# Layers' orders with seven stretches of tiled matmuls an item and two sets of squares, and a first attention with later loads and foldings among the scores

## The reference

```
xn = layernorm(x)
# branch 1: attention over all 512 tokens, 16 heads of 8 channels, interleaved rotary
q, k = rope(xn @ Wq.T), rope(xn @ Wk.T);  v = xn @ Wv.T
a = softmax(q k^T / sqrt(8)) v
# branch 2: six layers on y = xn
for i in range(6):
    # local attention: 16 heads of 64, windows of 32 queries that see 64 keys
    q, k, v = split(shift(y) @ Wqkv[i])        # shift: half of the channels one token later
    q, k = rotary(l2norm(q) * qs), rotary(l2norm(k) * ks)
    y = local_softmax(8 q k^T, masked) v @ Wo[i] + y
    # feed forward: layer norm, gelu gate, hidden size 341
    h = layernorm(shift(y)) * g + b
    y = (h @ W1a + b1a) * gelu(h @ W1g + b1g) @ W2[i] + b2 + y
out = x + a + y
```

## Time and profile before

| what | value |
|---|---|
| median of three runs | 3385.4 us |
| the profiled execution | 3384.84 us |
| its span, first to last instruction | 3383.0 us |
| granted TensorE clock, mean | 0.978 |
| first attention, to the layers' first load | 0 to 485.4 us |
| layers | 485.4 to 3383.0 us |

### The profile page before, as it was taken

The page is one execution under the profiler, slowest core; times in us unless marked ns, Lnnn a source line. Parts: engine busy times, 40 slices in busy tenths (PEclk is TensorE's granted clock), DMA queues, the critical chain, the costliest instruction groups (busy, mean ns, idle before and its releaser), DMA issues.

```text
span 3383.0 us, 96906 instructions
## 1 busy us (share of the span) xinstructions
PE 3228.3 (95%) x39772; PEld 1496.3 (44%) x39772; DVE 2841.0 (84%) x3719; ACT 1766.0 (52%) x2636; POOL 2647.8 (78%) x1918
## 2 busy tenths in 40 slices
PE   6899976899999999999999999999999999999988
PEld 4333232444444444444444444444444444444443
DVE  6899936888888888888888888888888888888863
ACT  2578853455555555545555555555555555555542
POOL 3223217999899999999999989989989999888961
PEclk7899997999999999999999999999999999999999
DMA  7333122333333333333333333333333333333321
GB/s 215 83 62 65 39 95 70 84 79 80 86 84 92 85 79 78 94 77 92 84 80 86 84 90 86 80 81 89 81 90 85 80 86 82 90 84 79 79 64 53
DMA packets 200487, 283.38 MB, mean 84 GB/s; under 512 B 56561, under 2 KB 82417, under 8 KB 199153
## 3 DMA queue, kind: packets, MB, share of 16 engines
q1 hardware_dynamic: 196304, 262.75, 31.6%
q10 hardware_dynamic: 3744, 14.43, 1.2%
HBM read 44.30 MB, written 19.55 MB: 19 GB/s over the span
## 4 chain that ended last, share of the span: by engine, by line
PE 78%; SPq 2%; POOL 2%; DVE 1%; issue 1%; DMA 1%; ACT 1%; DVEq 0%; POOLq 0%
PE ly_pj_ps L1005 20%; PE ly_to_ps L1081 20%; PE ly_pair_ps L1069 11%; PE ly_pair_ps L1049 9%; PE ly_to_ps L1111 4%; PE ly_pair_ps L1099 4%; PE ly_pair_ps L1103 3%; PE ly_nq_ps L1015 3%; PE ly_pair_ps L1036 2%; SPq L914 1%; PE ly_pair_ps L1089 1%; PE ly_pair_ps L1058 1%; SPq L904 1%; PE ly_pair_ps L1029 1%; DMA ly_kp<-ly_kr 0%
## 5 line engine op out<-in xcount | busy, mean ns | idle before, releaser
L1206 DVE SCALAR_TENSOR_TENSOR ly_prod<-ly_pj_ps,ly_few,ly_tables 128x1024 f32<-128x1024 f32 x768 | 964.9, 1272 | 149.4 <-ACT ly_sq L1403 132.2
L1005 PE MATMUL ly_pj_ps<-ly_xs,ly_wqk 128*128 128x512 f32 x1536 | 802.0, 625 | 30.6 <-DVE ly_prod L1206 14.8
L1081 PE MATMUL ly_to_ps<-ly_u,ly_mvo 128*128 128x512 f32 x1536 | 763.8, 606 | 0.9 <-issue 0.7
L1403 ACT ACTIVATE ly_sq<-ly_pj_ps 128x512 f32<-128x512 f32 x768 | 451.4, 603 | 574.7 <-PE ly_pj_ps L1005 494.1
L1499 POOL TENSOR_TENSOR ly_sq<-ly_sq 128x512 f32<-128x512 f32 x384 | 488.1, 1278 | 119.1 <-ACT ly_sq L1403 118.2
L1503 POOL TENSOR_TENSOR ly_sx<-ly_sx,ly_smax 128x1024 f32<-128x1024 f32 x192 | 365.7, 1905 | 126.0 <-DVE ly_smax L1282 125.5
L1434 ACT COPY ly_u<-ly_pair_ps 128x1024 f32<-128x1024 f32 x384 | 369.4, 1013 | 133.0 <-PE ly_pair_ps L1069 133.0
L1005 PEld LDWEIGHTS ly_pj_ps<-ly_xs,ly_wqk 128*128 128x128 f32 x1536 | 266.8, 192 | 347.7 <-issue 236.9
L1049 PEld LDWEIGHTS ly_pair_ps<-ly_kp,ly_qp 64*32 64x32 f32 x24576 | 277.4, 106 | 281.3 <-issue 242.6
L1081 PEld LDWEIGHTS ly_to_ps<-ly_u,ly_mvo 128*128 128x128 f32 x1536 | 272.6, 190 | 276.2 <-issue 262.9
L1069 PE MATMUL ly_pair_ps<-ly_pt,ly_xt 32*128 32x512 f32 x3072 | 385.3, 615 | 9.5 <-ACT ly_u L1434 6.8
(11 more groups left out here) (125 smaller groups left out, 4232.4 us busy)
## 6 DMA issues: line engine op xcount, KB each, us to landing
ly_qp<-ly_qr SPq DMA_DIRECT2D x1536, 64.0 KB
ly_kp<-ly_kr SPq DMA_DIRECT2D x1536, 64.0 KB, 2.0
ly_xt<-ly_xt SPq DMA_DIRECT2D x48, 192.0 KB
ga_parts_dram<-ga_parts SPq DMA_DIRECT2D x16, 384.0 KB, 2.4
ga_qs<-ga_parts_dram SPq DMA_DIRECT2D x96, 64.0 KB
ga_ks<-ga_parts_dram SPq DMA_DIRECT2D x96, 64.0 KB
ly_wqk<-in_wqk SPq DMA_DIRECT2D x24, 256.0 KB, 3.8
ly_mvo<-mvo_dram SPq DMA_DIRECT2D x24, 256.0 KB, 3.8
```

The source lines that it names most:

```text
L1005: pe.matmul(pj_ps[:, j % 2, :], wqk[:, g, j % TILES, :], xs[:, n % 2, WIN:], start=True, stop=True).then_inc(proj_ready.sem, 1)
L1081: last = pe.matmul(to_ps[:], mvo[:, 4 * (h // 4) + BESIDE[h % 4], :], u[:, :, :, h, :].rearrange("p t c q -> p (t c) q"), start=(h == 0), ...
L1206: dve.scalar_tensor_tensor(prod[:, k], pj_ps[:, j % 2, :].unsqueeze(1).to_broadcast([P, 2, N]), gains[:, n // B, k:k + 1], tables[:, table ...
L1403: act.activation(sq[:, k, :], pj_ps[:, j % 2, :], ACT.Square).then_inc(sq_done.sem, 1)
```

## The change

In the first attention, the load of items 4 to 7 (`load_x(2)`) moves from the start to behind item 0's stacking, and the raw weights of layer 1 are loaded by ACT only when item 0's stacked rows have landed. The items' normalising, turning and copying is split: items 1 to 3 in body 0, items 4 to 7 in body 1. The early foldings 4 to 15 move from body 0 (and 11 to 15 from body 1) to places among `first` of item 0 in body 1. The late foldings 17 to 23 stand among the scores of item 7 in body 9; before, 18 to 23 stood in body 10 after them. The store of an item's sum moves behind the late stores, and POOL waits for a group of x only where it adds it.

```diff
@@ first attention, SP
-            load_x(2)
...
+            def load_last_x(n):
+                if n == 0:
+                    load_x(2)
...
-                take_maxima(x_1, 0); stack(x_0, 1); store_sum(x_2); store_late(x_2, 0); store_late(x_2, 1)
+                take_maxima(x_1, 0); stack(x_0, 1); load_last_x(x_0); store_late(x_2, 0); store_late(x_2, 1); store_sum(x_2)
@@ first attention, PE (early and late foldings and the turns of the items)
+            def turn_group(n, g):
...
+                fold(x_0, 0); out(x_3, 3)
...
+                fold(x_0, 1); first(x_1, 3); second(x_2, 6); first(x_1, 4); meet(x_2, 1, 0); fold(x_2, 17); second(x_2, 7)
...
+                first(x_1, 5); meet(x_2, 1, 1); second(x_2, 8); first(x_1, 6); fold(x_1, 4); meet(x_2, 2, 0); second(x_2, 9)
+                fold(x_0, 2); fold(x_0, 3); turn_group(x_0, 1)
+                first(x_1, 7); fold(x_1, 5); meet(x_2, 2, 1); first(x_1, 8); fold(x_1, 6); second(x_2, 10); meet(x_2, 3, 0)
...
+                first(x_1, 9); fold(x_1, 7); out(x_2, 0); fold(x_2, 18); fold(x_2, 19); second(x_2, 12); first(x_1, 10)
+                turn_group(x_1, 2); meet(x_2, 4, 0)
...
+                meet(x_2, 5, 0); meet(x_2, 5, 1); fold(x_2, 20); first(x_1, 13); fold(x_1, 8); second(x_2, 15); meet(x_2, 6, 0)
...
+                fold(x_1, 9); second(x_2, 16)
+                meet(x_2, 6, 1); first(x_1, 15); fold(x_1, 10); second(x_2, 17); meet(x_2, 7, 0); meet(x_2, 7, 1); first(x_1, 16)
+                fold(x_1, 11)
+                second(x_2, 18); first(x_1, 17); meet(x_2, 8, 0); second(x_2, 19); out(x_2, 1); fold(x_2, 21); second(x_2, 20)
...
+                meet(x_2, 9, 0); fold(x_2, 22); fold(x_2, 23); second(x_2, 22); first(x_1, 20); meet(x_2, 9, 1)
...
+                second(x_2, 25); first(x_1, 23); fold(x_1, 12); meet(x_2, 11, 0); second(x_2, 26); first(x_1, 24); fold(x_1, 13)
...
+                first(x_1, 25); fold(x_1, 14); second(x_2, 28); first(x_1, 26); fold(x_1, 15); meet(x_2, 12, 0)
...
+                first(x_1, 27); meet(x_2, 13, 0); fold(x_1, 16); meet(x_2, 13, 1); second(x_2, 30); first(x_1, 28)
@@ first attention, ACT
-            load_raw(1)
...
+            def load_second_raw(n):
+                if n != 0:
+                    return
+                act.wait_ge(stacked[0].sem, stacked[0].at(0, 16 * 4 * len(TERMS)))
+                load_raw(1)
+
+                exponentials(x_2, 3, 4); take(x_3, 3); exponentials(x_2, 5, 6, 7, 8, 9, 10, 11, 12, 13, 14, 15)
+                gain_early(x_0, 0); take_early(x_0, 0); copy_values(x_0); take_early(x_0, 1); take_early(x_0, 2)
+                copy_group(x_0, 1)
+                load_second_raw(x_0); pass_on(x_0, 0)
+                gain_early(x_1, 1); take_early(x_1, 3); take_early(x_1, 4); take_early(x_1, 5); pass_on(x_1, 1)
+                copy_group(x_1, 2)
...
@@ first attention, DVE
...
+                maxima(x_1, 3, 4, 5, 6, 7, 8, 9); normalise_group(x_1, 2); take_late(x_2, 1); gain_late(x_2, 0); output(x_2, 0)
+                take_late(x_2, 2); gain_late(x_2, 1); take_late(x_2, 3); normalise_group(x_0, 1)
+                maxima(x_1, 10, 11, 12, 13, 14, 15, 16, 17); output(x_2, 1); take_late(x_2, 4); take_late(x_2, 5); maxima(x_1, 18)
...
@@ layers: two sets of squares (buffer, square_sums, squares, add_squares)
-        sq = sb("sq", [P, TILES, N])
+        sq = sb("sq", [P, 2, TILES, N])
+                        last = pe.matmul(nq_ps[32 * t:32 * t + 32, 0:P], heads[:, g, side, :], sq[:, g % 2, 2 * side, t * P:(t + 1) * P],
-                    if k == 0 and UNITS * n + g:
-                        act.wait_ge(ns_ready.sem, UNITS * n + g)
-                    act.activation(sq[:, k, :], pj_ps[:, j % 2, :], ACT.Square).then_inc(sq_done.sem, 1)
+                    if k == 0 and UNITS * n + g >= 2:
+                        act.wait_ge(ns_ready.sem, UNITS * n + g - 1)
+                    act.activation(sq[:, g % 2, k, :], pj_ps[:, j % 2, :], ACT.Square).then_inc(sq_done.sem, 1)
+                    side, at = k // 2 % 2, 2 * (k % 2)
+                    pool.tensor_tensor(sq[:, side, at], sq[:, side, at], sq[:, side, at + 1], ALU.add).then_inc(sq_added.sem, 1)
```

More of the change, by code:

```diff
@@ L428, in body @@
[L428 to L431, removed]
@@ L673, in _ @@
             pool.memset(ks[:].bitcast(F32), ONE_PAIR).then_inc(ks_set, 1)
-            for g in range(len(GROUPS_LN)):
-                pool.wait_ge(x_in[g], 16)
             def cut_sums(n, i):
@@ L707, in add_tokens @@
                     return
+                for g, (first, _) in enumerate(GROUPS_LN):
+                    if n == first:
+                        pool.wait_ge(x_in[g], 16)
                 pool.wait_ge(out_steps.sem, out_steps.at(n, 8))
@@ L1182, in body @@
+                if x_6 is not None: turn_ffn_tokens(x_6)
+                if x_7 is not None: up_value(x_7, 2); down(x_7, 1)
+                if x_3 is not None: project(x_3, 10)
+                if x_5 is not None: attend(x_5, 2)
+                if x_3 is not None: square_sums(x_3, 1); project(x_3, 11, 12)
+                if x_5 is not None: attend(x_5, 3)
+                if x_3 is not None: project(x_3, 13)
                 if x_7 is not None: down(x_7, 2)
-                if x_5 is not None: attend(x_5, 2)
@@ L1184, in body @@
-                if x_3 is not None: square_sums(x_3, 2); project(x_3, 12, 13)
-                if x_5 is not None: attend(x_5, 3)
-                if x_3 is not None: project(x_3, 14)
                 if i == ITEMS + 5: turn_back(0, 1)
@@ L1349, in body @@
                 if x_7 is not None: normalise(x_7)
+                if x_5 is not None: prob_sums(x_5, 2); inverse_sums(x_5, 2)
+                if i == ITEMS + 6: add_sums(2)
                 if x_3 is not None: products(x_3, 1)
+                if x_4 is not None: scale_keys(x_4, 1)
+                if x_5 is not None: prob_sums(x_5, 3); prob_blocks(x_5, 2); inverse_sums(x_5, 3)
+                if x_3 is not None: products(x_3, 2)
+                if x_7 is not None: gated(x_7, 0)
+                if x_3 is not None: products(x_3, 3)
@@ L1351, in body @@
+                if x_7 is not None: gated(x_7, 1)
+                if x_4 is not None: scale_keys(x_4, 2)
                 if i == ITEMS + 6: add_sums(3)
-                if x_4 is not None: scale_keys(x_4, 1)
-                if x_5 is not None: prob_sums(x_5, 3); inverse_sums(x_5, 3); prob_blocks(x_5, 2)
-                if x_7 is not None: gated(x_7, 0)
-                if x_3 is not None: products(x_3, 2)
                 if x_5 is not None: prob_blocks(x_5, 3)
-                if x_7 is not None: gated(x_7, 1)
@@ L1368, in body @@
[L1368 to L1372 removed]
+                if x_3 is not None: products(x_3, 9)
+                if x_6 is not None: token_moments(x_6)
+                if x_3 is not None: products(x_3, 10)
+                if x_4 is not None: prob_sums(x_4, 0)
@@ L1376, in body @@
-                if x_3 is not None: products(x_3, 12)
+                if x_4 is not None: mask_scores(x_4, 2); score_maxima(x_4, 2)
+                if x_3 is not None: products(x_3, 14, 15)
             bodies(body)
@@ L1457, in body @@
-                if x_7 is not None: ffn_tokens(x_7)
-                if x_6 is not None: take_u(x_6, 6, 7)
-                if x_4 is not None: squares(x_4, 14, 15); copy_sums(x_4)
+                if x_6 is not None: take_u(x_6, 6)
+                if x_4 is not None: squares(x_4, 13)
+                if x_6 is not None: take_u(x_6, 7)
+                if x_4 is not None: squares(x_4, 14, 15)
                 if x_3 is not None: tokens(x_3)
-                if x_5 is not None: exponentials(x_5, 2)
```

241 lines of the change are left out of this document (107 added, 134 removed).

## The result

Four executions of the changed kernel gave 3425.29 to 3447.81 us, median 3431.1 us; the kernel before, run beside them, 3384.6 us. The ratio is 1.014 (95% interval 1.011 to 1.017): slower by 1.4%, where 3290 us was forecast. The profiled execution took 3425.29 us.

The account below looks back on a forecast made before the run. PE's own time was taken to bound the layers. From 3384.8 us, 76 saved in the layers (1.65 us an item, 46 items) and 19 in the first attention gave 3290 us, range 3260 to 3328.

Parts of the forecast that it names:

- Step 1: Layers, PE: 15 stretches of tiled matmuls become 7, fewer entry and exit surcharges, 1.45 us an item saved.
- Step 2: Layers, scores of units 0 and 1: four touching halves take 0.70 us each instead of 0.79, saving 0.27 us an item.
- Step 3: Layers, four joints of tile shapes: charged like leaving the stretch, no change; bounds 0.5 us saved, 0.4 us lost.
- Step 4: Layers: other engines follow at 56.2 us an item, nothing late; 0.1 us added for slips, 56.3.
- the nine tight places: Layers: nine places where data is ready only 0.5 to 1 us before it is wanted.
- The prediction's own sign for the main step: Layers: PE showing waits of over 1 us an item would mean the main step is wrong.
- First attention, start: Item 0: with other traffic held, the keys' parts are back at 32.3 us and scores start 19 us earlier.
- Body 1: First attention: layer norm of four items adds 11 us on DVE, of which the moved foldings give back 5.
- End: End of first attention: late foldings lengthen item 7 by 3 us, the tail vanishes; 6 us gained, ends 0 and 9.
- Rival D: Layers, unit 1's scores: keys late by 3 us, item 59.2 us, slower at 3426 us; chance 0.04.
- rival E: Layers: surcharge goes with the kind of pass, not the stretch; nothing saved there, 3366 us; chance 0.02.

Follow-up runs that it names:

- e1: Changed kernel with one move, combine 14 between the two units of scores, so 128 passes touch instead of 256: 3403.6 us, 1.0056 of before.
- e5: Changed kernel with the first attention of before, three combine between the scores of units 0 and 1, attend 0 and DVE's order adapted: 3415.8 us, 1.0095.
- e11: As e5, with project 7 ahead of spread_norms 3, project 8 ahead of attend 1, product 2 and ACT's squares 6 to 8 moved ahead: 3433.1 us, 1.016.
- e7: Kernel before, with both parts of item 0 sent on SP before either is stacked: 3383.8 us, 0.9993.
- e9: Changed kernel's first attention with layers of before, but early foldings at their old places and layer 1's raw weights loaded at the start: 3397.9 us, 1.005.
- e8: Changed kernel's first attention with layers of before, but x of items 4 to 7 loaded at the start, their layer norm in body 0: 3384.4 us, 1.0008.
- e6: Kernel before, with only the late foldings (17 to 23) among item 7's scores and the sum stored last: 3382.6 us, 0.9997.
- e12: As e11, with combine 13 and prob_blocks 2 put back, so combine 14 and 15 stand between the scores of units 0 and 1: 3371.1 us, 0.9975.
- e13: As e12, with project 5 also between the scores of units 0 and 1, and gated 1 ahead of product 3 on DVE: 3351.0 us, 0.991.
- e10: Changed kernel with ten further PE waits a body on counts long reached, which became five instructions: 3461 us in its one execution.

## Why the prediction was wrong, by its steps

- Step 1, right. The halves and the square sums at joints took what was forecast: a scores half ahead of a square sum 0.79, the square sum 0.57, a pair of passes ahead of tiled ones 0.95. The passes outside the tiled stretches, as distances between starts, took 39.71 us in the median item, before 41.19: 1.48 less, where 1.45 was forecast. In the mean it is 1.2, since later items have further gaps among them.
- Step 2, the failed one: "Four halves in a row", 0.70 each. The rate was right (128 passes in 1.41 us in e1), but 256 such passes want 512 instructions in 2.8 us, and PE got them only with a stop of 2.1 us. The stretch took 4.97 us (median) instead of 2.9. Not the cost of a pass was wrong but what bounds it: PE's time was taken as the only limit in the layers, and the supply of its instructions was put at nothing. I priced a run of small passes by its weight loads and never asked who delivers the instructions. The term was -0.27 us an item and measured +1.81 (4.97 less four times 0.79).
- Step 3, right. Joints inside a stretch paid like leaving it.
- Step 4, right for data as far as it was put to the test: the nine tight places gave PE 2.3 us of waits in 2400. But with the stop 56.2 was not PE's pace, and a stop in front of them loosens the places behind it: in e1, with half of it gone, `attend` 0 waited. That tight places are real is what e5 and e11 show, where the two new waits of each cost 1.8 and 1.4 us an item. The prediction's own sign for the main step, waits of PE of over 1 us an item, came: 84.3 us in 41 items, 2.1 each.
- First attention, start: 6.6 us gained of 19. "Back at 32.3" was wrong; the parts took 9.4 us though, from 29.5 to 39 us, no other data moved than they and the stackings (ACT's queue has no packet there). They were issued behind 12 stackings in the same queue, and sent ahead of them (e7) nothing waits for them. What held traffic did save is the time of the stackings.
- Body 1: 27.7 us more, where 6 were taken. Layer norm 9, near the 11 worked out, but DVE did not stand idle elsewhere as I took it. The foldings were put down as a relief; among the maxima they cost 14 to 21, as e9 and e8 bound it. That each hands a bank to ACT and back while PE's next scores stand behind it is the reading of the ACT rows above; no run takes the handing over away alone.
- End: the tail from the last exponentials to the layers' first load shrank from 17.9 us to 7.2, and the last item's exponentials grew from 37.8 to 45.6: 2.9 gained of 6, and in e6 nothing that the time shows. Another 4.6 us were lost between body 1 and this end; the cause stays open.

The miss by parts, from the traces: the layers took 2915.0 us from DVE's first instruction to the end, before 2897.3, forecast 2821, so 94 us too few; the first attention ended 42 us later than forecast (508.2 against 466). Step 2's term alone, 2.08 us an item against its forecast, is 96 us in 46 items.

Rival D had the sign by another mechanism: it saw late keys, for which PE waited 0.2 us in all. None of the rivals was about the supply of instructions, and rival E, for the layers, is refuted by step 1's 1.48 us.

## What to carry to other kernels

A row of busy time prices a pass only at the density at which it was seen: before merging runs of very short instructions, count the instructions and ask at which rate the engine gets them, and leave slow passes between. A gap of an engine put down to "issue" that walks by a fixed number of instructions an item and always ends the same time after a transfer of instructions lands is its instruction supply, not data. Work that hands a bank to another engine and back can be a poor filler among passes that need the next bank; here it lengthened them.

## What the runs showed of the hardware

- PE's instructions arrive during the run in blocks of 256 (16.4 KB; 318 transfers for 81473 instructions). A gap that waits for one ended 1.1 to 1.6 us after it landed (46 of 46 in the changed kernel), and no two of the transfers of that execution started less than 3.27 us apart.
- In e1 the first 128 small passes in a row, which have only slow ones ahead of them for long, ran without a gap in every item (1.41 to 1.66 us); the second 128, 1.05 us later, were stopped in nearly every one. 256 in a row were stopped in all of 41 items, with 1.7 to 3.0 us between the starts of two passes. The kernel before, whose runs are of 64, had 12 such waits in 41 items, of 0.8 us at most.
- With nothing, 1.05, 1.9 and 2.8 us of slow passes between the two halves (the changed kernel, e1, e12, e13), the gaps inside the scores were 2.32, 1.26, 0.37 and 0.21 us an item; in e12 and e13 another 0.3 fell in the square sum behind them.
- In e10 two blocks in a row inside the stretch stopped 3.4 and 4.1 us after one another (1565.99 - 1562.57 and 1570.11 - 1565.99), so in a long run small passes get 128 in 3.4 to 4.1 us. How far ahead PE's instructions are brought, and what a transfer waits for, no run here shows.
- Instructions of PE that only wait for counts long met cost nothing at their place: in e10 the two passes ahead of the five take 0.95 us as without them, and the scores behind them 0.79. The item of 59.33 us against 58.48 (one profile each) comes from longer gaps in and around the scores and from waits for products just ahead of them.
